# Second layer: value projection with gated weights and the gate's diagonal; VectorE adds the residual base

## Chip, core and metric

The kernel runs on one core of one Trainium2 chip. The metric is the device time of one execution in microseconds. The engines are TensorE (PE, matmuls into PSUM; PEld is its weight load), VectorE (DVE), ScalarE (ACT), GpSimd (POOL), and SyncE, whose queue (SPq) issues the DMAs.

## What is computed

Two transformer layers over x of 32 sequences, 256 tokens, 128 features, float32. The part that the change touches is the attention of the second layer:

```python
h = _layernorm(x, axis=-1) * (1 + ca) + sa
x = x + ga * _L1_attn_ref(h, ...)          # ga, ca, sa: one row of 128 for each sequence

def _L1_attn_ref(x, ln_scale, ln_bias, wq, wk, wv):
    xn = _layernorm(x, ln_scale, ln_bias)
    q, k, v = ((xn @ w) split in 16 heads of 8 for w in (wq, wk, wv))
    probs = softmax(q @ k.T / sqrt(128))
    return heads_joined(probs @ v) + xn    # the residual inside the attention is xn
```

So with x as it enters the layer, the new x is x + ga·(probs @ v) + ga·xn. The first layer has another attention (an output projection, a slope bias, no inner residual). A mixture of experts follows each attention; its input rows are written by token to a table in DRAM.

## The kernel before

The program has five blocks in time: setup (constants, the modulation rows of both layers), attention of layer 0, experts 0, attention of layer 1, experts 1. An attention block is a software pipeline over the 32 sequences. One **tick** `i` works on several sequences at once: `at(off)` is sequence `i + off`. Each engine has a hand-written order of steps within a tick (`tick` in each engine's block); the first and the last ticks are peeled, the middle runs in a loop of two ticks. Engines wait for each other by counting semaphores. A `Signal` is one such count, and `after(b)` is its value once sequence `b` is through.

TensorE's tick has 16 score passes `scores_a` (L1093, one for each head, into the two PSUM tiles `A`), of which VectorE takes the row maxima (`row_max`, L849). Pass h may start when maximum h - 2 has been taken. Between the passes stand the transposed scores `scores_b` (L1117), the sums `weigh` (L1132) and small steps that share the one PSUM bank `M0`: `project_qk` (L1076, L1077), `project_v` (L1081), transposes, router products. ScalarE takes the exponentials (L701) and reads `M0` into SBUF; `values` (L686) reads the projected values.

The attention of layer 1 has these steps around the change:

- GpSimd `add_experts` (L577 to L579) makes X, the input of layer 1, from the first layer's rows; it runs three sequences ahead.
- VectorE `outer_norm` (the L803 group that writes xn from X, two instructions), `modulate_rows` (L832, L834) and `inner_norm` (L803, xn from xn) make the normalised rows, two sequences ahead. TensorE turns them; ScalarE applies `ln_scale` and `ln_bias` and writes hT, the transposed xn of the reference.
- GpSimd `split_qk` (L567 to L570, four instructions of 512 columns) and then `residual_base` (L588 to L591, four of 256 columns) run one sequence ahead. `residual_base` computes X + ga·(xn·ln_scale + ln_bias) into `xh`; `store_base` (L490) sends it to DRAM and `load_back` (L485) brings it back as `XR` when it is needed.
- VectorE `residual` (L890, L892), two sequences behind, computes h3 = On·ga + XR, where On holds the attention's output.

The SP queue issues, in a fixed order in each tick, 12 DMAs of 64 KB for the score stacks (`stack<-parts`, L498), 2 for the maxima (`stack<-mrow`, L504), and the loads and stores of rows. It waits in order: what stands behind a waiting issue waits too.

Of the kernel before, what the change touches and what calls it, by code (L numbers as in the profile page):

```python
# [40 lines left out]
DVE_MARKS = (36, 42)  # L41
# [81 lines left out]
def build(nc, a, out):  # L123
    with ExitStack() as ctx:
# [6 lines left out]
        def dram(name, shape, dt=F32):  # L131
# [4 lines left out]

        x_mid = [dram(f"x_mid{n}", (B * S, D)) for n in range(3)]
# [19 lines left out]
        wo = sb("wo", [P, P])  # L157
        qk_bias = sb("qk_bias", [P, 2])
# [46 lines left out]
        xh = [sb(f"xh{u}", [P, NT, D]) for u in range(2)]  # L205
        gb_row = [sb(f"gb_row{u}", [P, 1, D]) for u in range(2)]
        lnrow = sb("lnrow", [P, 2, D])
# [53 lines left out]
            (ln_cols[:, :], a["ln_cols"]), (lnrow[:, :, :], a["ln_rows"].broadcast_to([P, 2, D])), (gate_w[:, :, :], a["gate_w"]), (cT[:, :, :], a["cT"]),  # L261
# [130 lines left out]
def attention(nc, l, g):  # L392

    (X, XR, X1, st, mv, rs, xn, hT, qk, rem, parts, stack, vals, mx, mneg, mrow, probs, heads, rsum, On, OnT, yT,
     st2, mv2, rs2, xn2, front_rows, back_rows, xh, qs_bias, h2, h3, h2T, eps_col, lg, rt, r1, sel, slot_in, token_ids, run) = (g[n] for n in (
        "X XR X1 st mv rs xn hT qk rem parts stack vals mx mneg mrow probs heads rsum On OnT yT "
        "st2 mv2 rs2 xn2 front_rows back_rows xh qs_bias h2 h3 h2T eps_col lg rt r1 sel slot_in token_ids run").split())
# [6 lines left out]
    gb_row, ones_col, lnrow, Y, expert_out, XR, a, w1, w2, b1, b2 = (g[n] for n in  # L404
        "gb_row ones_col lnrow Y expert_out XR a w1 w2 b1 b2".split())
# [19 lines left out]
    back_in = transfers("back_in", 2)  # L425
    base_out = transfers("base_out", 1)
# [30 lines left out]
    with nc.Block() as block:  # L457

        @block.sync
        def _(sp):  # L460
# [7 lines left out]
            def load_front(b, k, u):  # L468
# [3 lines left out]
                else:  # L472
                    sp.wait_ge(base_ready.handle, base_ready.after(b - 2))
# [3 lines left out]
                    sp.dma_start(front_rows[u][:, :, :], mod_of(1, b, SA, 3)).then_inc(front_in[u], 16)  # L477
# [1155 lines left out]
```

## Time and profile before

| | |
|---|---|
| median of 3 runs | 2274.51 us (2273.72 to 2276.03) |
| profiled execution, its own time | 2273.52 us |
| its span in the trace | 2271.7 us |
| busy share PE / DVE / ACT / POOL | 79% / 75% / 46% / 42% |
| setup | 0 to about 41 us |
| attention 0 | about 42 to 890 us |
| experts 0 | about 890 to 1137 us |
| attention 1 | about 1155 to 2000 us |
| experts 1 | about 2020 to 2271 us |

How to read what is quoted: a window row gives start and end, then the busy time of PE, PEld, DVE, ACT and POOL in this order, each with its count of instructions, then the granted TensorE clock as a share of full speed, the busy share of the DMA engines, and GB/s. A group row gives a line of the kernel, the engine, the operation, its output and inputs with shapes, the count, the busy time, the mean in ns, and the idle time just before. A timeline row gives start and duration in us; "x2" means that the row stands for two instructions in a row, and a bracket is idle time before it and who ended it.

### The profile page before, as it was taken

How to read it: one execution, taken by the hardware profiler on the slowest of the kernel's cores; microseconds unless marked ns; L12 is line 12 of the kernel's file. 1: busy time of each engine (PE TensorE's matmuls, PEld its weight loads, DVE VectorE, ACT ScalarE, POOL GpSimd, SP SyncE). 2: the span in 40 equal slices, each digit the busy share in tenths (PEclk: the TensorE clock that was granted, in tenths of full speed). 3: DMA queues.
4: the chain of work that ended last, by engine and by line, in shares of the span. 5: the costliest groups of instructions: out<-in, count | busy, mean ns of one | idle time of the engine just before them, and what ended most of it. 6: DMA issues, size and time to landing. Idle time of an engine off the chain costs nothing. (4 is left out here: it accounts for less than half of the span.)

```text
span 2271.7 us, 57921 instructions
## 1 busy us (share of the span) xinstructions
PE 1787.5 (79%) x15650; PEld 1288.8 (57%) x15650; DVE 1694.5 (75%) x5861; ACT 1039.5 (46%) x1967; POOL 951.4 (42%) x1028
## 2 busy tenths in 40 slices
PE   1699999999999929999906777777777777719997
PEld 1466666666667618999803444444444444407776
DVE  3488888888888746666627988998999899824453
ACT  0266666666666612222204555555555555602322
POOL 0233444343444324454425455445545554313433
PEclk7699999999999969999957999999999998959999
DMA  3334444444444332222235443544444444343332
GB/s 125 48 69 70 75 74 76 70 76 71 75 73 73 61 72 59 71 69 67 60 115 90 100 98 91 98 101 100 94 99 98 96 96 95 70 141 96 100 92 62
DMA packets 260822, 191.15 MB, mean 84 GB/s; under 512 B 24824, under 2 KB 251002, under 8 KB 260046
## 3 DMA queue, kind: packets, MB, share of 16 engines
q1 hardware_dynamic: 245402, 155.40, 33.2%
q0 software_dynamic: 15360, 35.03, 5.4%
q8 instruction: 28, 0.46, 0.1%
q14 instruction: 32, 0.26, 0.1%
HBM read 95.37 MB, written 53.15 MB: 65 GB/s over the span
## 5 line engine op out<-in xcount | busy, mean ns | idle before, releaser
L849 DVE TENSOR_REDUCE mx<-A 128x2 f32<-128x512 f32 x1024 | 692.6, 683 | 127.5 <-PE A L1097 51.1
L701 ACT ACTIVATE probs<-B 128x1024 f32<-128x1024 f32 x512 | 524.0, 1023 | 350.4 <-PE B L1120 180.8
L1093 PE MATMUL A<-stack 126*128 126x256 bf16 x2048 | 440.7, 287 | 159.6 <-DVE mx L849 127.9
L1117 PE MATMUL B<-stack 128*128 128x256 bf16 x2048 | 364.1, 281 | 31.8 <-DMA stack<-mrow 31.6
L1093 PEld LDWEIGHTS A<-stack 126*128 126x128 bf16 x2048 | 180.8, 100 | 328.9 <-DVE mx L849 244.4
L1132 PE MATMUL M<-probs,vals 128*32 128x256 f32 x4096 | 289.1, 399 | 21.6 <-DVE On L875 17.4
L611 POOL DMA_INDIRECT gathered<-h,slot_in x192 | 187.2, 975 | 155.2 <-DVE slot_in L988 109.6
L1117 PEld LDWEIGHTS B<-stack 128*128 128x128 bf16 x2048 | 203.4, 103 | 83.2 <-issue 31.2
L598 POOL TENSOR_TENSOR h<-xn,back_rows 128x256 f32<-128x256 f32 x64 | 46.4, 724 | 465.6 <-DVE xn L803 465.6
L1533 PE MATMUL A<-w2s,hid 128*128 128x128 f32 x1792 | 230.5, 279 | 9.0 <-issue 9.0
L1533 PEld LDWEIGHTS A<-w2s,hid 128*128 128x128 f32 x1792 | 211.9, 192 | 18.3 <-issue 13.3
L1524 PE MATMUL B<-xtT,w1s 128*128 128x256 f32 x896 | 216.3, 395 | 6.0 <-DVE xtT L1410 2.8
L1339 POOL DMA_INDIRECT expert_out<-yt,row_dest x144 | 138.1, 959 | 177.7 <-DVE yt L1445 143.4
L1097 PE MATMUL A<-dist,slope_ident 128*128 128x128 bf16 x1024 | 201.2, 222 | 0.0
L1524 PEld LDWEIGHTS B<-xtT,w1s 128*128 128x128 f32 x896 | 168.3, 195 | 40.5 <-issue 17.1
L1132 PEld LDWEIGHTS M<-probs,vals 128*32 128x32 f32 x4096 | 125.1, 112 | 103.4 <-issue 43.4
L1120 PE MATMUL B<-dist,slope_ident 128*128 128x128 bf16 x1024 | 183.1, 219 | 0.0
L1493 ACT ACTIVATE hid<-B 128x1024 f32<-128x1024 f32 x72 | 73.7, 1024 | 228.7 <-PE B L1524 228.7
L567 POOL TENSOR_TENSOR parts<-qk,ones_col 128x512 bf16<-128x512 f32 x64 | 66.5, 1039 | 258.8 <-ACT qk L680 112.5
L708 ACT ACTIVATE heads<-M 128x256 f32<-128x256 f32 x256 | 97.9, 382 | 147.7 <-PE M L1132 146.7
L1336 POOL DMA_INDIRECT out<-yt,row_dest x80 | 84.5, 1056 | 169.7 <-DVE yt L1450 146.2
L1497 ACT ACTIVATE hid<-B,b 128x256 f32<-128x256 f32 x160 | 62.6, 474 | 173.4 <-PE B L1524 138.0
(193 smaller groups left out, 3079.2 us busy)
## 6 DMA issues: line engine op xcount, KB each, us to landing
stack<-parts SPq DMA_DIRECT2D x768, 64.0 KB
xt<-gathered SPq DMA_DIRECT2D x112, 132.0 KB, 2.2
back_rows<-mod_rows SPq DMA_DIRECT2D x64, 192.0 KB, 3.4
probs<-gathered SPq DMA_DIRECT2D x40, 256.0 KB, 2.7
w<-in_w SPq DMA_DIRECT2D x4, 2048.0 KB
Y<-expert_out SPq DMA_DIRECT2D x64, 128.0 KB
front_rows<-mod_rows SPq DMA_DIRECT2D x32, 192.0 KB
X<-in_x SPq DMA_DIRECT2D x32, 128.0 KB, 3.2
```

What stands on the lines that cost most here:

```text
L611: pool.indirect_dma_start(gathered[l], bass.IndirectOffsetOnAxis(ap=slot_in[u][:, c, t:t + 1], axis=0), (h3 if l else h2)[u][:, t, :], Non ...
L701: act.activation(probs[c % 4][:, :, :, :], Bp[c % 2][:, :, :, :], ACT.Exp, scale=EXP_SCALE[l][c // 4]).then_inc(b_exp.handle, 1)
L708: act.activation(heads[g % 2][:, :], M1[:, 0:S], ACT.Copy).then_inc(o_read.handle, 1)
L849: dve.tensor_reduce(mx[u][:, h, :], A[h % 2][:, :, :], AX.X, ALU.max).then_inc(a_max.handle, 1)
L1093: ins = pe.matmul(A[h % 2][:, t, :], stack[u][0:n, h, 0, t * P:(t + 1) * P], stack[u][0:n, h, 1, :], start=True, stop=(l == 1))
L1097: ins = pe.matmul(A[h % 2][:, t, t * P:(t + 1) * P], slope_ident[:, h % HH, :], dist[:, t, :], start=False, stop=True)
L1117: ins = pe.matmul(Bp[c % 2][:, j, t, :], stack[u][:, h, 1, t * P:(t + 1) * P], stack[u][:, h, 0, :], start=True, stop=(l == 1))
L1120: ins = pe.matmul(Bp[c % 2][:, j, t, t * P:(t + 1) * P], slope_ident[:, h % HH, :], dist[:, 1 - t, :], start=False, stop=True)
L1132: ins = pe.matmul(M1[VW * j:VW * j + VW, 0:S], vals[u][:, t, 4 * g + j, :], probs[(2 * g + j // 2) % 4][:, j % 2, t, :], start=(t == 0), s ...
L1339: ins = pool.indirect_dma_start(expert_out[l], dest, yt[u][:, t, :], None)
L1524: ins = pe.matmul(dst[:, f, :], w1s[u][:, f * P:(f + 1) * P], xtT[u][:, :], start=True, stop=True)
L1533: ins = pe.matmul(A[u][:, t, 0:D], hid[u][:, f, t * P:(t + 1) * P], w2s[u][:, f, :], start=(f == 0), stop=(l == 0 and f == FC - 1))
```

## The change

`residual_base`, `store_base` and the tiles `xh` and `lnrow` go. In their place:

- **Setup**: the gate rows ga go to a DRAM table `gate_rows` of 32 x 256, the right half in plain order, the left half in the order in which the heads stand (three DMAs at the end of the setup block, and a wait for them). A constant `wv_id` of 128 x 256 (wv beside the identity) is loaded instead of `lnrow`.
- **SP queue**: `load_ga` brings the row of a sequence, broadcast to 128 partitions; `store_x2` sends X to DRAM and `load_x2` brings it back as `XR`, in place of `xh`. `back_rows` and `front_rows` lose a row each.
- **GpSimd** `gate_values`: one product of 128 x 256, `wv_ga = wv_id * ga_rows`: the value weights and the identity with every column multiplied by ga.
- **TensorE** `project_v`: 256 columns instead of 128 for each half of the sequence. `M0` then holds ga·v and beside it ga·xn, and all 512 columns are in use.
- **VectorE** `gated_base`: xb = XR + the right halves of `M0`, after `modulate_rows`. `residual` becomes one addition, On + xb. TensorE's next users of `M0` (`count`, `turn_max`) wait for `base_ready` instead of `v_ready`.

```diff
@@ setup, SP queue
+                sp.dma_start(gate_rows[:, D:2 * D], mod_sb[:, GA * D:(GA + 1) * D]).then_inc(gates_out, 16)
+                for f in range(2):
+                    sp.dma_start(gate_rows[:, f * (D // 2):(f + 1) * (D // 2)].rearrange("b (h d) -> b h d", d=HD),
+                                 mod_sb[:, GA * D:(GA + 1) * D].rearrange("b (h f d) -> b f h d", f=2, d=HD)[:, f, :, :])\
+                        .then_inc(gates_out, 16)
+                sp.wait_ge(gates_out, 48)
...
@@ attention, SP queue
-                    sp.wait_ge(base_ready.handle, base_ready.after(b - 2))
+                    sp.wait_ge(h_rows.handle, h_rows.after(b - 2))
+                    sp.wait_ge(x2_out[u], x2_out.of(k - 1))
                     sp.dma_start(X[u][:, :, :], rows_of(x_view[1], b)).then_inc(x_in[u], 16)
...
-                if l == 1:
-                    sp.wait_ge(base_out[u], base_out.of(k))
-                sp.dma_start(XR[u][:, :, :], rows_of(x_view[2 * l], b)).then_inc(back_in[u], 16)
-                sp.dma_start(back_rows[u][:, :, :], mod_of(l, b, GA, 3)).then_inc(back_in[u], 16)
-
-            def store_base(b, k, u):
-                sp.wait_ge(base_ready.handle, base_ready.after(b))
-                sp.dma_start(rows_of(x_view[2], b), xh[u][:, :, :]).then_inc(base_out[u], 16)
+                if l == 0:
+                    sp.dma_start(XR[u][:, :, :], rows_of(x_view[0], b)).then_inc(back_in[u], 16)
+                sp.dma_start(back_rows[u][:, 1:3, :], mod_of(l, b, SB, 2)).then_inc(back_in[u], 16)
+
+            def store_x2(b, k, u):
+                sp.wait_ge(x2_ready.handle, x2_ready.after(b))
+                sp.dma_start(rows_of(x_view[2], b), X[u][:, :, :]).then_inc(x2_out[u], 16)
+
+            def load_x2(b, k, u):
+                sp.wait_ge(base_ready.handle, base_ready.after(b - 2))
+                sp.wait_ge(x2_out[u], x2_out.of(k))
+                sp.dma_start(XR[u][:, :, :], rows_of(x_view[2], b)).then_inc(x2_in[u], 16)
+
+            def load_ga(b, k, u):
+                sp.wait_ge(wv_ready.handle, wv_ready.after(b - 2))
+                sp.dma_start(ga_rows[u][:, :], gate_rows[bass.ds(b, 1), :].broadcast_to([P, 2 * D])).then_inc(ga_in[u], 16)
...
                     stack_max(*at(-1), 1)
+                if l and at(2):
+                    store_x2(*at(2))
+                    load_ga(*at(2))
                 if at(-1):
                     load_back(*at(-1))
...
                 if l and at(1):
-                    store_base(*at(1))
+                    load_x2(*at(1))
...
@@ attention, GpSimd
-            def residual_base(b, k, u):
-
-                def row(n, x):
-                    return x[:, n:n + 1, :].broadcast_to([P, NT, D])
-                pool.wait_ge(xn_ready.handle, xn_ready.after(b))
-                pool.wait_ge(base_out[u], base_out.of(k - 1))
-                h = xh[u][:, :, :]
-                ch.link(pool.tensor_tensor(h, xn[u][:, :, :], row(0, lnrow), ALU.mult))
-                ch.link(pool.tensor_tensor(h, h, row(1, lnrow), ALU.add))
-                ch.link(pool.tensor_tensor(h, h, row(GA, front_rows[u]), ALU.mult))
-                pool.tensor_tensor(h, h, X[u][:, :, :], ALU.add).then_inc(base_ready.handle, 1)
+            def gate_values(b, k, u):
+                pool.wait_ge(ga_in[u], ga_in.of(k))
+                pool.wait_ge(v_proj.handle, v_proj.after(b - 2))
+                pool.tensor_tensor(wv_ga[u][:, :], wv_id[:, :], ga_rows[u][:, :], ALU.mult).then_inc(wv_ready.handle, 1)
...
@@ attention, VectorE
+            def gated_base(b, k, u):
+
+                dve.wait_ge(x2_in[u], x2_in.of(k))
+                dve.wait_ge(v_ready.handle, v_ready.after(b))
+                dve.wait_ge(x1_ready.handle, x1_ready.after(b - 2))
+                dve.tensor_tensor(xb[u][:, :, :], XR[u][:, :, :],
+                                  M0[:, :].rearrange("p (t n) -> p t n", t=NT)[:, :, D:2 * D], ALU.add)\
+                    .then_inc(base_ready.handle, 1)
+
             def residual(b, k, u):
...
-                    x3 = x1_of(u)
-                    ch.link(dve.tensor_tensor(x3, On[u][:, :, :, :].rearrange("p t h d -> p t (h d)"),
-                                              back_rows[u][:, 0:1, :].broadcast_to([P, NT, D]), ALU.mult))
-                    dve.tensor_tensor(x3, x3, XR[u][:, :, :], ALU.add).then_inc(x1_ready.handle, 1)
+                    dve.tensor_tensor(x1_of(u), On[u][:, :, :, :].rearrange("p t h d -> p t (h d)"), xb[u][:, :, :],
+                                      ALU.add).then_inc(x1_ready.handle, 1)
...
                 layer(1, modulate_rows, 2)
+                layer(1, gated_base, 0)
                 maxima(9, 1)
...
@@ attention, TensorE
             def project_v(b, k, u):
+                if l:
+                    pe.wait_ge(wv_ready.handle, wv_ready.after(b))
+                n, w = (2 * D, wv_ga[u][:, :]) if l else (D, wv[:, l, :])
                 for t in range(NT):
-                    ins = pe.matmul(M0[:, t * P:(t + 1) * P], hT[u][:, t * P:(t + 1) * P], wv[:, l, :],
-                                    start=True, stop=True)
+                    ins = pe.matmul(M0[:, t * n:(t + 1) * n], hT[u][:, t * P:(t + 1) * P], w, start=True, stop=True)
                 ins.then_inc(v_proj.handle, 1)
...
-                    m0_read(*[(x1_ready, -2)] * (l == 0), (v_ready, 0), (mT_read, -1, 2))
+                    m0_read(*[(x1_ready, -2)] * (l == 0), (base_ready if l else v_ready, 0), (mT_read, -1, 2))
...
-                    m0_read((pos_read, -3), *[(x1_ready, -2)] * (l == 0), (v_ready, 0))
+                    m0_read((pos_read, -3), *[(x1_ready, -2)] * (l == 0), (base_ready if l else v_ready, 0))
```

VectorE in the middle of a tick, before the change, from the residual (L890, L892) over two row maxima (L849) and statistics (h is the tile that takes the new x, mv and rs are mean and reciprocal deviation) to `outer_norm` (L803):

```order
L890 TENSOR_TENSOR h<-On,back_rows 128x2x128
L892 TENSOR_TENSOR h<-h,XR 128x2x128
L849 TENSOR_REDUCE mx<-A 128x2
L798 BN_STATS st<-h 128x6 x2
L849 TENSOR_REDUCE mx<-A 128x2
L789 BN_AGGR mv<-st 128x2 x2
L803 TENSOR_SCALAR xn<-X,mv,rs 128x128 x2
L856 TENSOR_SCALAR mneg<-mx 128x2x8
```

The same place after it (the line numbers are now those of the changed kernel):

```order
L916 TENSOR_TENSOR h<-On,xb 128x2x128
L867 TENSOR_REDUCE mx<-A 128x2
L817 BN_STATS st<-h 128x6 x2
L867 TENSOR_REDUCE mx<-A 128x2
L808 BN_AGGR mv<-st 128x2 x2
L822 TENSOR_SCALAR xn<-X,mv,rs 128x128 x2
L874 TENSOR_SCALAR mneg<-mx 128x2x8
```

One instruction has gone, and the others keep their order. A little later on VectorE, before, where the heads' output is normalised (On) and `modulate_rows` (L832, L834) is followed by the tenth row maximum:

```order
L871 RECIPROCAL rsum<-M 128x8
L875 TENSOR_TENSOR On<-M,rsum 128x2x4x8
L832 TENSOR_TENSOR xn<-xn,front_rows 128x256
L834 TENSOR_TENSOR xn<-xn,front_rows 128x256
L849 TENSOR_REDUCE mx<-A 128x2
L943 TENSOR_SCALAR h<-token_ids 128x2
```

And after:

```order
L889 RECIPROCAL rsum<-M 128x8
L893 TENSOR_TENSOR On<-M,rsum 128x2x4x8
L850 TENSOR_TENSOR xn<-xn,front_rows 128x256
L852 TENSOR_TENSOR xn<-xn,front_rows 128x256
L906 TENSOR_TENSOR xb<-XR,M 128x256
L867 TENSOR_REDUCE mx<-A 128x2
L969 TENSOR_SCALAR h<-token_ids 128x2
```

The new addition L906 stands ahead of the maximum. GpSimd's tick before, from the last two instructions of the split (parts and rem hold q and k and what bf16 leaves over) on:

```order
L569 TENSOR_TENSOR parts<-rem,ones_col 128x2x256
L99 REGISTER_ALU
L570 TENSOR_TENSOR parts<-rem,parts 128x2x256
L586 REGISTER_ALU
L588 TENSOR_TENSOR xh<-xn,lnrow 128x256
L99 REGISTER_ALU
L589 TENSOR_TENSOR xh<-xh,lnrow 128x256
L99 REGISTER_ALU
L590 TENSOR_TENSOR xh<-xh,front_rows 128x256
L99 REGISTER_ALU
L591 TENSOR_TENSOR xh<-xh,X 128x256
```

And after:

```order
L594 TENSOR_TENSOR parts<-rem,ones_col 128x2x256
L99 REGISTER_ALU
L595 TENSOR_TENSOR parts<-rem,parts 128x2x256
L607 ISA
L608 REGISTER_ALU
L609 TENSOR_TENSOR wv_ga<-wv_id,ga_rows 128x256
L613 REGISTER_ALU
L614 ISA
```

Of four instructions behind the split, one is left.

## Rows read from the trace of the kernel before

**Rows 1.** windows: start:end, length, busy us (count) each engine, PEclk, DMA

```profile
150.00:900.00 750.00, 665.54 (x7052) 493.78 (x7049) 615.78 (x2138) 422.22 (x771) 309.03 (x318) 0.97 0.40 71
...
1200.00:1900.00 700.00, 520.86 (x4445) 308.10 (x4445) 626.85 (x2009) 386.21 (x771) 361.46 (x418) 0.93 0.45 96
```

**Rows 2.** waits, 1250 to 1900 us: total us, times, longest us

```profile
PE A L1093 <- DVE mx L849: 89.1, 135, 1.7
...
DVE mx L849 <- PE A L1093: 32.0, 53, 0.7
```

**Rows 3.** DVE groups, 1250 to 1900 us: count, busy us, mean ns, idle us

```profile
L849 DVE TENSOR_REDUCE mx<-A 128x2 f32<-128x512 f32 x417 | 280.7, 678 | 35.4 <-PE A L1093 32.0
L803 DVE TENSOR_SCALAR xn<-X,mv,rs 128x128 f32<-128x128 f32 x52 | 39.4, 798 | 3.4
L890 DVE TENSOR_TENSOR h<-On,back_rows 128x256 f32<-128x256 f32 x26 | 32.5, 1251 | 1.4
L892 DVE TENSOR_TENSOR h<-h,XR 128x256 f32<-128x256 f32 x26 | 29.8, 1146 | 0.9
```

**Rows 4.** timeline of DVE in one tick: start us, duration us, instruction

```profile
1440.78 1.13 DVE L890 TENSOR_TENSOR h<-On,back_rows 128x256 f32<-128x256 f32 x1
1441.94 1.15 DVE L892 TENSOR_TENSOR h<-h,XR 128x256 f32<-128x256 f32 x1
1443.01 0.68 DVE L849 TENSOR_REDUCE mx<-A 128x2 f32<-128x512 f32 x1
...
1444.95 1.52 DVE L803 TENSOR_SCALAR xn<-X,mv,rs 128x128 f32<-128x128 f32 x2
...
1447.97 0.42 DVE L834 TENSOR_TENSOR xn<-xn,front_rows 128x256 f32<-128x256 f32 x1
```

**Rows 5.** timeline of POOL in the same tick

```profile
1440.47 1.16 POOL L568 TENSOR_TENSOR rem<-qk,parts 128x512 f32<-128x512 f32 x1
1441.70 1.10 POOL L569 TENSOR_TENSOR parts<-rem,ones_col 128x512 bf16<-128x512 f32 x1
1442.88 1.22 POOL L570 TENSOR_TENSOR parts<-rem,parts 128x512 bf16<-128x512 f32 x1
...
1444.86 0.72 POOL L589 TENSOR_TENSOR xh<-xh,lnrow 128x256 f32<-128x256 f32 x1
1445.67 0.72 POOL L590 TENSOR_TENSOR xh<-xh,front_rows 128x256 f32<-128x256 f32 x1
```

**Rows 6.** line 892, whole trace: durations min/median/max ns; its second last tick

```profile
L892 DVE TENSOR_TENSOR h<-h,XR x32: 424/1145/1273, 1242.9 to 1992.8; 128x256 f32<-128x256 f32 x32
...
1978.56 0.42 DVE L892 TENSOR_TENSOR h<-h,XR 128x256 f32<-128x256 f32 x1
```

**Rows 7.** lines 803 and 896 in the first layer, same columns

```profile
L803 DVE TENSOR_SCALAR xn<-X,mv,rs x106: 334/340/576, 202.8 to 812.7; 128x128 f32<-128x128 f32 x106
...
L896 DVE TENSOR_TENSOR X<-XR,M x28: 409/410/421, 219.7 to 809.3; 128x256 f32<-128x256 f32 x28
```

**Rows 8.** timeline of PE: a 256-column projection, and the tick of rows 4

```profile
1412.28 0.70 PE L1076 MATMUL M<-hT,wq 128*128 128x256 f32 x2
...
1442.78 0.61 PE L1081 MATMUL M<-wv,hT 128*128 128x128 f32 x4
...
1447.21 0.39 PE L1093 MATMUL A<-stack 126*128 126x256 bf16 x2 [1.65 <-DVE mx L849]
```

**Rows 9.** timeline of ACT in the tick of rows 4

```profile
1443.90 0.38 ACT L686 ACTIVATE vals<-M 128x256 f32<-128x256 f32 x1
```

**Rows 10.** waits of the SP queue, 1250 to 1900 us, and its stack issue

```profile
SPq L504 <- ACT mrow L694: 252.8, 52, 5.0
...
1419.48 4.00 SPq L498 DMA_DIRECT2D stack<-parts  x6
```

**Rows 11.** end of setup: timeline

```profile
38.70 0.33 SPq L281 DMA_DIRECT2D mod_rows<-mod_sb  x1
...
41.76 1.28 ACT L643 ACT_TABLE_LOAD   x1 [25.93 <-PEq L271]
```

More of the change, by code:

```diff
@@ L40 @@
 EPS_IN = 1e-6
-DVE_MARKS = (36, 42)
+DVE_MARKS = (36, 41)
 MIDST = (2, 4, 5, 7, 8, 10, 11, 13, 14)
@@ L204, in build @@
         back_rows = [sb(f"back_rows{u}", [P, 3, D]) for u in range(2)]
-        xh = [sb(f"xh{u}", [P, NT, D]) for u in range(2)]
+        xb = [sb(f"xb{u}", [P, NT, D]) for u in range(2)]
         gb_row = [sb(f"gb_row{u}", [P, 1, D]) for u in range(2)]
-        lnrow = sb("lnrow", [P, 2, D])
+        ga_rows = [sb(f"ga_rows{u}", [P, 2 * D]) for u in range(2)]
+        wv_ga = [sb(f"wv_ga{u}", [P, 2 * D]) for u in range(2)]
         h2 = [sb(f"h2{u}", [P, NT, W]) for u in range(2)]
@@ L403, in attention @@
         "before_tri ones_b rev_iota mod_rows gathered x_view region_row".split())
-    gb_row, ones_col, lnrow, Y, expert_out, XR, a, w1, w2, b1, b2 = (g[n] for n in
-        "gb_row ones_col lnrow Y expert_out XR a w1 w2 b1 b2".split())
+    gate_rows, ga_rows, wv_ga, wv_id = (g[n] for n in "gate_rows ga_rows wv_ga wv_id".split())
+    gb_row, ones_col, Y, expert_out, XR, a, w1, w2, b1, b2 = (g[n] for n in
+        "gb_row ones_col Y expert_out XR a w1 w2 b1 b2".split())
     n_choice = CHOICES[l]
@@ L424, in attention @@
     front_in = transfers("front_in", 4)
-    back_in = transfers("back_in", 2)
-    base_out = transfers("base_out", 1)
+    back_in = transfers("back_in", 1 if l else 2)
+    x2_out = transfers("x2_out", 1)
+    x2_in = transfers("x2_in", 1)
+    ga_in = transfers("ga_in", 1)
     stack_in = Transfers([[sem(f"stack_in{u}{h}") for h in range(2)] for u in range(2)], len(PRODUCTS))
@@ L523, in _ @@
                 sp.wait_ge(lin_in, 32)
-            for t in (x_in, stack_in, m_in, x1_out, front_in, back_in, base_out, gate_in):
+            for t in (x_in, stack_in, m_in, x1_out, front_in, back_in, x2_out, x2_in, ga_in, gate_in):
                 t.start(sp)
@@ L551, in _ @@
             for u in range(2):
-                sp.wait_ge(*((base_out[u], base_out.of(B // 2 - 1)) if l else (x1_out[u], x1_out.of(B // 2 - 1))))
+                sp.wait_ge(*((x2_in[u], x2_in.of(B // 2 - 1)) if l else (x1_out[u], x1_out.of(B // 2 - 1))))
         @block.gpsimd
         def _(pool):
-            start(pool, split, h2_ready, scattered, *([base_ready, x2_ready] if l else []))
+            start(pool, split, h2_ready, scattered, *([wv_ready, x2_ready] if l else []))
             ch = Chain(pool, pool_order)
@@ L632, in tick @@
                     scatter_done(*at(-3))
-            run_ticks(pool, tick, ch, 10 if l else 5)
+            run_ticks(pool, tick, ch, 7 if l else 5)
         @block.scalar
@@ L780, in _ @@
             if l == 1:
-                start(dve, h_rows, h_stats, rms_stats, h3_ready)
+                start(dve, h_rows, h_stats, rms_stats, h3_ready, base_ready)
             ch = Chain(dve, dve_order)
@@ L826, in outer_norm @@
                 dve.wait_ge(xn_T.handle, xn_T.after(b - 2))
-                dve.wait_ge(base_ready.handle, base_ready.after(b - 2))
                 normed(X[u], mv[u], rs[u], xn[u], h_rows)
```

27 lines of the change are left out of this document (16 added, 11 removed).

## The prediction, made before the changed kernel was timed

> **What bounds the kernel now.** First the windows [rows 1]. In the attention of layer 1 VectorE is busy 626.85 of 700 us (90%), TensorE 74%, ScalarE 55%, GpSimd 52%. A tick is short to see: 417 row maxima in 650 us [rows 3], 16 to a tick, make 26.1 ticks, so 24.9 us each. Then the waits [rows 2]: in this stretch TensorE waits 89.1 us for row maxima, VectorE 32.0 us for scores. So the tick is VectorE's list of work, with TensorE close behind in places. The change touches only this block and the end of setup; layer 0 loses one row of 64 KB from a load that nobody waits for.
>
> Then the groups of VectorE [rows 3]. Two instructions of 256 columns in `residual`, L890 and L892, take 1251 and 1146 ns each, and the two of 128 columns in `outer_norm` (L803 from X) 798 ns. The same shapes are much cheaper elsewhere: L892 takes 0.42 us in the last ticks, where GpSimd has no split [rows 6], and L803 a median of 340 ns in layer 0 [rows 7]. The two timelines beside each other say why [rows 4, 5]: L890 starts at 1440.78, while GpSimd's L568 runs until 1441.63, and ends at 1441.91, 0.28 behind it. L892 ends at 1443.09, 0.29 behind L569 (1442.80). The pair of `outer_norm` starts at 1444.95 inside L589 (until 1445.58) and ends at 1446.47, just behind L590 (1446.39). Each of these four instructions stands until the GpSimd instruction beside it is over. The row maxima keep their 678 ns. What an edit to either engine is worth hangs on who meets whom.
>
> **The change part by part.** The sum is made against the profiled execution, 2273.52 us (span 2271.7 and 1.8 around it), which is 1.0 us below the median.
>
> *L892 goes.* In rows 4 the next maximum starts at 1443.01, 0.08 before the end of L892. Behind L890 alone (end 1441.91) it would start at 1441.83: 1.18 us earlier. Its operands are there: its score pass stands before the heads' product in TensorE's order. What is left of `residual` starts where L890 did and meets the same L568, so it keeps its 1.13 us. Of the 32 instructions I count 29 as blocked and 3 at 0.46 with the gap (the last ticks, [rows 6]): 29 x 1.18 + 3 x 0.46 = 35.6 us less.
>
> *`outer_norm` meets other GpSimd work.* It starts 1.18 earlier, at 1443.77. L570 then still runs, until 1444.10 at the latest [rows 5], perhaps 0.1 less since nothing pushes it. Behind it GpSimd now has one product of 256 columns, to be priced as L589: 0.72 us, from 1444.08 to 1444.80. So the first half of `outer_norm` waits for L570, the second for the product, and the pair ends about 0.08 behind it, at 1444.88: 1.11 us instead of 1.52, 0.41 less. The bounds: nothing gained (1.52 again), or both free, 2 x 0.34 with an overlap [rows 7], 0.9 less. I take 0.41, as the four starts in rows 4 and 5 fix it. In 29 ticks: 11.9 us less.
>
> *`gated_base` is added.* The nearest row is L896 of layer 0: the same shape, one operand in SBUF and one in PSUM, 410 ns with a spread of 409 to 421 [rows 7]. With the spacing of such a step 0.44 us, 32 times: 14.1 us more. If it too were held up by a GpSimd instruction it would take what L892 takes, 1.15 us, and 29 x 0.74 = 21.5 us more again. I take the lower: it comes just behind L834 (end 1448.39, [rows 4], now about 1.6 earlier), and GpSimd would be idle from 1444.80 on. The Trainium skill ("SBUF — State Buffer", section "Who interferes with whom") says that a VectorE instruction with two SBUF inputs contends with a GpSimd instruction that reads SBUF, and one with at most one SBUF input outside the two-port modes does not. By that rule the 21.5 us can't come even if the two meet; rows 3 to 5 agree with its first half, and no row here shows the second, since I found L896 beside no GpSimd arithmetic.
>
> Does `gated_base` wait? It needs `values` of ScalarE, which ended at 1444.28 [rows 9]. The wider projection makes that later: L1081 took 0.61 us for two tiles of 128 columns, L1076 0.70 for one of 256 [rows 8], so two take at most 1.40: at most 0.8 later, 1445.1. VectorE comes to it at about 1446.8. No wait. Its other inputs come from transfers a tick older.
>
> *TensorE.* Those 0.8 us stand between `scores_b` and the ninth score pass. In rows 8 the projection starts at 1442.78, so it ends by 1444.18, and the pass (0.39 us) by 1444.57. The maximum that reads it was taken behind `outer_norm`, which now ends at 1444.88. Hidden, by 0.3 us; before the change TensorE had 1.65 us of idle two passes on [rows 8]. The new wait of `count` and `turn_max` for `base_ready` costs nothing: VectorE has passed `gated_base` before it takes the tenth maximum, and both stand behind a score pass that needs the eleventh.
>
> *GpSimd* loses three instructions of 0.72 us in each tick. It is no bound; the only worth of it is in `outer_norm`, above.
>
> *The SP queue* issues one transfer more in each tick (x2 out and in for base out and in, and the gate row), some 0.35 to 0.5 us, ahead of the stack issue of 4.00 us [rows 10]. The queue stands idle 4.9 us twice in each tick before a `stack<-mrow` (252.8 us over 52, [rows 10]): covered. `store_x2` makes the queue wait for `add_experts`, with the stack rows of the next sequence behind it; GpSimd has done that at the end of the tick before.
>
> *Setup.* The last transfer of the modulation rows is issued at 38.70, and attention 0 begins at 41.76 [rows 11]: 3.06 us from issue to the next block. Three more are issued only after its landing, 0.33 each at the least and, in pieces of 8 elements, 0.67 each as one stack transfer (4.00 over six, [rows 10]), and must land: about 1.7 + 2.3 = 4.0 us more, between 2.5 and 8. Nothing else runs there.
>
> Sum: -35.6 - 11.9 + 14.1 + 4.0 = -29.4 us; 2273.5 - 29.4 = 2244.1, by the median 2245.
>
> **The rivals.**
>
> A. As above, with the bounds of `outer_norm`: nothing gained there gives 2257, all of it (29 x 0.49 more) 2231. Chance 0.68.
>
> B. More than that. TensorE's long wait of 1.65 us shrinks, and its clock, granted at 0.93 on average in this block [rows 1], stays high; VectorE's own 32 us of waits [rows 2] is then halved: 16 less, 2215 to 2230. For it: the idle does shrink. Against: most of these waits are elsewhere in the tick. Chance 0.08.
>
> C. VectorE gives the time back. The stretch from the heads' product to the ninth pass is full of TensorE work, and the margin found above is 0.3 us. If the pass comes 0.5 us later than worked out, 0.2 to 0.5 of the 1.15 us a tick is lost, or `gated_base` is blocked (0.74 a tick): 2257 to 2270. Chance 0.13.
>
> D. The change doesn't do what it says: the gain of a tick is eaten, because TensorE's path, not VectorE, sets the time from L890 to the ninth pass. Then L892's going is worth nothing there, and what is left is +0.44 and -0.41 a tick and the setup: 2270 to 2279, within 0.2%. Against: TensorE waits for a maximum at both ends of this stretch. Chance 0.05.
>
> E. Slower. The same place, with TensorE the bound behind the wider projection: +0.8 us a tick for it, and nothing from L892 and `outer_norm`: 32 x 0.8 - 3 + 4 = +27, with `gated_base` hidden in VectorE's new idle; 2290 to 2310. It decides once the ninth pass ends later than VectorE asks for it; it stands 0.4 us short of that by the numbers above, and would have to come 1.5 us later to use up the gain. For it: the stretch has no gap in TensorE. Against: the 1.65 us. Chance 0.06.
>
> **How the numbers follow.** About 0.2% (4.5 us) is what a measurement of this kernel can tell from no change. Faster by more: A, B and C, 0.89, less a little for a C that reaches 2270: 0.88. Same: D with that remainder, 0.06. Slower: 0.06. The range is 2228, just inside B, to 2263, half-way through C: it holds A whole and parts of both, some 0.8.
>
> **What would show it.** In the groups of VectorE: no L892, the one instruction of `residual` at 1.1 to 1.25 us still, `outer_norm` at some 0.55 us each, `gated_base` at 0.41 without a wait before it. The tick, from one residual to the next over two ticks, 23.8 us instead of 24.9. VectorE still at 90%, TensorE at 80% with its waits for maxima down. Attention 0 begins at some 45.8. The prediction is wrong if VectorE's idle before maxima grows by what its work shrinks (C, D, E), if `outer_norm` keeps 798 ns (A's upper end), or if `gated_base` stands for `values` or takes over 1 us.

## Result, and the profile after

The changed kernel takes 2248.83 us (median of 4 runs, 2240.77 to 2250.82) against 2274.95 us beside it: ratio 0.9879 (95% interval 0.9853 to 0.9904), 26 us less. Two later comparisons on other occasions gave 0.9867 (0.9852 to 0.9882) and 0.9872 (0.9855 to 0.9888). The forecast was 2245, with 2228 to 2263.

The profiled execution took 2240.77 us, the least of the four, with a span of 2239.0: 32.7 us below the span of before. Measured by the starts of the `residual` instruction over 26 ticks in the middle of attention 1, a tick fell from 24.99 to 23.84 us.

The window of attention 1, as in [rows 1] (660 us, since the block is shorter):

```profile
1200.00:1860.00 660.00, 508.50 (x4389) 299.66 (x4387) 584.46 (x1989) 379.73 (x761) 292.80 (x327) 0.95 0.51 102
```

VectorE is busy 584.46 of 660 us (89%), TensorE 77% instead of 74%, GpSimd 44% instead of 52%. The waits, as in [rows 2], over 600 us instead of 650:

```profile
PE A L1122 <- DVE mx L867: 65.2, 98, 0.9
...
DVE mx L867 <- PE A L1122: 32.3, 51, 0.9
```

TensorE's waits for row maxima fell from 3.4 to 2.6 us a tick; VectorE's waits for scores are 1.28 us a tick, where they were 1.23. VectorE is the bound as before, of a shorter list. VectorE's groups, as in [rows 3], 1250 to 1850 us:

```profile
L867 DVE TENSOR_REDUCE mx<-A 128x2 f32<-128x512 f32 x404 | 271.6, 677 | 32.5 <-PE A L1122 32.3
L916 DVE TENSOR_TENSOR h<-On,xb 128x256 f32<-128x256 f32 x25 | 32.2, 1287 | 0.6
L822 DVE TENSOR_SCALAR xn<-X,mv,rs 128x128 f32<-128x128 f32 x50 | 27.6, 591 | 1.5
...
L852 DVE TENSOR_TENSOR xn<-xn,front_rows 128x256 f32<-128x256 f32 x25 | 10.6, 425 | 0.9
L906 DVE TENSOR_TENSOR xb<-XR,M 128x256 f32<-128x256 f32 x25 | 10.5, 421 | 5.7 <-DVE xn L852 5.7
```

The residual's one instruction (L916) is held up as L890 was, 1287 ns against 1251. `outer_norm` (L822 from X) fell from 798 to 591 ns. `gated_base` (L906) takes 421 ns; the 0.23 us of idle time before it (5.7 over 25 of them) are put down to VectorE's own L852, so it waited for no other engine. One tick of VectorE, as in [rows 4]:

```profile
1621.13 1.17 DVE L916 TENSOR_TENSOR h<-On,xb 128x256 f32<-128x256 f32 x1
1622.22 0.68 DVE L867 TENSOR_REDUCE mx<-A 128x2 f32<-128x512 f32 x1
...
1624.10 1.10 DVE L822 TENSOR_SCALAR xn<-X,mv,rs 128x128 f32<-128x128 f32 x2
...
1626.70 0.43 DVE L852 TENSOR_TENSOR xn<-xn,front_rows 128x256 f32<-128x256 f32 x1
1627.35 0.42 DVE L906 TENSOR_TENSOR xb<-XR,M 128x256 f32<-128x256 f32 x1 [0.23 <-DVE xn L852]
1627.69 0.68 DVE L867 TENSOR_REDUCE mx<-A 128x2 f32<-128x512 f32 x1
```

And GpSimd in the same tick, as in [rows 5]:

```profile
1620.86 1.16 POOL L593 TENSOR_TENSOR rem<-qk,parts 128x512 f32<-128x512 f32 x1
1622.09 1.10 POOL L594 TENSOR_TENSOR parts<-rem,ones_col 128x512 bf16<-128x512 f32 x1
1623.27 1.16 POOL L595 TENSOR_TENSOR parts<-rem,parts 128x512 bf16<-128x512 f32 x1
1624.39 0.72 POOL L609 TENSOR_TENSOR wv_ga<-wv_id,ga_rows 128x256 f32<-128x256 f32 x1
```

L916 ends at 1622.30, 0.28 behind L593 (1622.02). `outer_norm` starts at 1624.10 inside L595 (until 1624.43) and ends at 1625.20, 0.09 behind the gate product (1625.11); from single instructions, its first half ends 0.08 behind L595 and its second 0.08 behind the product. From the start of L852 to the start of the next maximum it is 0.99 us (1626.70 to 1627.69). Before, without `gated_base`, it was 0.55 from L834 (1447.97, [rows 4]) to the maximum behind it:

```profile
1448.52 0.69 DVE L849 TENSOR_REDUCE mx<-A 128x2 f32<-128x512 f32 x1
```

So `gated_base` adds 0.44. TensorE and ScalarE in the same tick, as in [rows 8, 9]:

```profile
1623.13 1.03 PE L1111 MATMUL M<-wv_ga,hT 128*128 128x256 f32 x4
1623.99 0.38 PE L1122 MATMUL A<-stack 126*128 126x256 bf16 x2
...
1625.93 0.39 PE L1122 MATMUL A<-stack 126*128 126x256 bf16 x2 [0.61 <-DVE mx L867]
```

```profile
1624.25 0.38 ACT L706 ACTIVATE vals<-M 128x256 f32<-128x256 f32 x1
```

The projection L1111 takes 1.03 us for 0.61, and the ninth pass starts at 1623.99 behind it with no wait for VectorE. `values` ends at 1624.63, 2.7 us before `gated_base`. The end of setup, as in [rows 11]:

```profile
38.84 0.33 SPq L285 DMA_DIRECT2D mod_rows<-mod_sb  x1
...
40.63 0.32 SPq L287 DMA_DIRECT2D gate_rows<-mod_sb  x1
40.98 0.92 SPq L289 DMA_DIRECT2D gate_rows<-mod_sb  x2
44.36 1.28 ACT L661 ACT_TABLE_LOAD   x1 [28.50 <-PEq L275]
```

The three gate transfers are issued from 40.63 to 41.90, and the block begins at 44.36 instead of 41.76. In the other traces of kernels with this setup it begins between 43.69 and 44.11.

### The profile page after: what moved, and what is told of

Same layout as the page of the kernel before. It is cut to its first block and busy times, and to the rows that moved or that the text cites. A ratio compares the mean times of both kernels' runs of the same rounds, so it can differ in the third digit from the quotient of the medians.

```text
span 2239.0 us, 57857 instructions
## 1 busy us (share of the span) xinstructions
PE 1779.3 (79%) x15650; PEld 1283.3 (57%) x15650; DVE 1652.0 (74%) x5861; ACT 1039.1 (46%) x1967; POOL 881.2 (39%) x932
## 5 line engine op out<-in xcount | busy, mean ns | idle before, releaser
L1122 PE MATMUL A<-stack 126*128 126x256 bf16 x2048 | 433.2, 283 | 136.2 <-DVE mx L867 102.5
L1146 PE MATMUL B<-stack 128*128 128x256 bf16 x2048 | 357.7, 277 | 32.6 <-DMA stack<-mrow 32.4
L1146 PEld LDWEIGHTS B<-stack 128*128 128x128 bf16 x2048 | 197.2, 101 | 84.3 <-issue 30.6
```

What stands on the lines that cost most here:

```text
L1122: ins = pe.matmul(A[h % 2][:, t, :], stack[u][0:n, h, 0, t * P:(t + 1) * P], stack[u][0:n, h, 1, :], start=True, stop=(l == 1))
L1146: ins = pe.matmul(Bp[c % 2][:, j, t, :], stack[u][:, h, 1, t * P:(t + 1) * P], stack[u][:, h, 0, :], start=True, stop=(l == 1))
```

## Experiments

Each was timed beside the kernel before on the same chip; "tick" is the mean over 26 middle ticks, read from its trace as above. The first four ran on another chip, where every kernel takes some 130 us more: the kernel before 2407.34 us. Most of that lies in layer 0, whose attention ended at 958 to 962 us in the four traces of that chip, instead of 832 to 835; the cause was not looked for. (The table ahead of the change puts the end of attention 0 at about 890. In the trace of before its last row maximum ends at 787.5, and VectorE's first instruction of experts 0 starts at 831.9; that is the point meant here.) Attention 1 is alike there (a variant of the changed kernel, e4 below, has a tick of 23.88 us), so ticks can be compared, and times only as ratios.

**The kernel before without L890 (e1).**

```diff
-                    ch.link(dve.tensor_tensor(x3, On..., back_rows..., ALU.mult))
-                    dve.tensor_tensor(x3, x3, XR[u][:, :, :], ALU.add).then_inc(x1_ready.handle, 1)
+                    dve.tensor_tensor(x3, On..., XR[u][:, :, :], ALU.add).then_inc(x1_ready.handle, 1)
```

This leaves the gate out of the attention's part. (Operands are cut to `...`.)

> The kernel before with one edit: the product On*ga (L890) is left out, so the residual is the single addition On + XR; GpSimd's four instructions of the residual base stay. Theory (each of VectorE's two-input or two-port instructions stands until the GpSimd instruction beside it ends, and the tick is VectorE's list): the residual loses one instruction of 1.18 us a tick (35 us), and outer_norm, which then starts 1.18 us earlier, waits for L570 and for L588 alone instead of L589 and L590: 1.11 us for its pair instead of 1.52, 12 us more; 2227 us. Rival 1 (outer_norm got shorter because GpSimd's list did): it keeps 1.5 us and the time is 2239. Rival 2 (TensorE sets this stretch): above 2260.

Measured: 2383.03 us, ratio 0.9910 (0.9892 to 0.9929), 24 us less; tick 24.16, so 0.83 less and not 1.6. The groups of VectorE, 1350 to 1950 us:

```profile
L890 DVE TENSOR_TENSOR h<-On,XR 128x256 f32<-128x256 f32 x24 | 30.3, 1262 | 1.3
L803 DVE TENSOR_SCALAR xn<-X,mv,rs 128x128 f32<-128x128 f32 x50 | 26.6, 572 | 3.0
...
L834 DVE TENSOR_TENSOR xn<-xn,front_rows 128x256 f32<-128x256 f32 x25 | 21.0, 839 | 0.9
...
L832 DVE TENSOR_TENSOR xn<-xn,front_rows 128x256 f32<-128x256 f32 x25 | 18.8, 752 | 0.0
```

The two things expected are there: one residual instruction at 1262 ns, and `outer_norm` at 572 ns with all four GpSimd instructions in place, so rival 1 falls: it got shorter because it comes earlier. But `modulate_rows` (L832, L834) takes 752 and 839 ns: VectorE, ahead by 1.6 us, has run into L590 and L591. Before, from 1250 to 1900 us:

```profile
L834 DVE TENSOR_TENSOR xn<-xn,front_rows 128x256 f32<-128x256 f32 x26 | 11.0, 425 | 0.9
L832 DVE TENSOR_TENSOR xn<-xn,front_rows 128x256 f32<-128x256 f32 x26 | 10.8, 415 | 0.0
```

That is 0.75 us a tick more: 1.18 + 0.45 - 0.75 = 0.88, for 0.83 measured.

**The kernel before with one GpSimd instruction as residual base (e2).**

```diff
-                ch.link(pool.tensor_tensor(h, xn[u][:, :, :], row(0, lnrow), ALU.mult))
-                ch.link(pool.tensor_tensor(h, h, row(1, lnrow), ALU.add))
-                ch.link(pool.tensor_tensor(h, h, row(GA, front_rows[u]), ALU.mult))
-                pool.tensor_tensor(h, h, X[u][:, :, :], ALU.add).then_inc(base_ready.handle, 1)
+                pool.tensor_tensor(h, xn[u][:, :, :], X[u][:, :, :], ALU.add).then_inc(base_ready.handle, 1)
```

This leaves the scale, bias and gate out of the base. 

> The kernel before with one edit: GpSimd's residual base is one instruction of 256 columns (xn + X) instead of four; VectorE's list is untouched. Theory: the residual keeps its 1.13 to 1.38 and 1.15 us, but outer_norm, which starts 0.15 us after that one instruction has ended, runs free at 0.6 us for the pair instead of 1.52: 0.9 us a tick, 26 us less, 2249 us. Rival (a lighter GpSimd list is worth nothing): 2275 us. In between, 0.3 to 0.6 us a tick, if the one instruction still touches the pair: 2258 to 2266.

Measured: 2383.02 us, ratio 0.9908 (0.9890 to 0.9926); tick 24.16, 0.83 less. The same groups:

```profile
L887 DVE TENSOR_TENSOR h<-On,back_rows 128x256 f32<-128x256 f32 x25 | 30.5, 1220 | 1.4
L889 DVE TENSOR_TENSOR h<-h,XR 128x256 f32<-128x256 f32 x24 | 27.5, 1146 | 0.8
...
L800 DVE TENSOR_SCALAR xn<-X,mv,rs 128x128 f32<-128x128 f32 x50 | 16.3, 369 | 3.0
```

The residual is as it was, and `outer_norm` takes 369 ns, 0.86 us a tick less. Nothing was taken from VectorE's list: GpSimd instructions that GpSimd had ample time for cost VectorE 0.86 us a tick where they met it.

**More GpSimd products beside `gated_base`, in the changed kernel (e3).**

```diff
+                for _ in range(5):
+                    ch.link(pool.tensor_tensor(beside[:, :], wv_id[:, :], wv_id[:, :], ALU.mult))
```

(`beside` is a tile of its own that nothing reads.)

> The changed kernel with five more GpSimd products of 256 columns (0.72 us each, SBUF to SBUF, result unused) behind the gate product, so that GpSimd computes from 1624.4 to about 1629.2 in the tick shown, over modulate_rows and gated_base. Theory (two SBUF inputs are held up, one in SBUF and one in PSUM is not): L850 and L852 take about 0.7 to 0.9 us each instead of 0.42, gated_base (L906) keeps 0.41 to 0.43; some 0.75 us a tick, 22 us more than the changed kernel, 2271 us. Rival (gated_base is held up too): L906 at 0.7 to 1.1 us and 2280 to 2290 us.

Measured: 2405.15 us, ratio 1.0004 (0.9988 to 1.0019), against 0.988 for the changed kernel: 30 us more (by the ratios; e4 below, which takes what the changed kernel does, took 2375.35 us on this chip); tick 24.94, 1.10 more. That is more than the 22 us of the theory and close to the rival's, so the groups have to decide. VectorE's groups, then the five products of one tick on GpSimd, then VectorE beside them:

```profile
L877 DVE TENSOR_SCALAR mneg<-mx 128x16 bf16<-128x16 f32 x49 | 20.4, 417 | 4.2 <-issue 4.0
...
L855 DVE TENSOR_TENSOR xn<-xn,front_rows 128x256 f32<-128x256 f32 x25 | 18.0, 719 | 0.9
L853 DVE TENSOR_TENSOR xn<-xn,front_rows 128x256 f32<-128x256 f32 x25 | 16.0, 642 | 0.0
...
L909 DVE TENSOR_TENSOR xb<-XR,M 128x256 f32<-128x256 f32 x25 | 10.5, 422 | 5.3 <-DVE xn L855 5.3
```

```profile
1720.11 3.50 POOL L612 TENSOR_TENSOR beside<-wv_id 128x256 f32<-128x256 f32 x5
```

```profile
1722.42 0.72 DVE L855 TENSOR_TENSOR xn<-xn,front_rows 128x256 f32<-128x256 f32 x1
1723.37 0.42 DVE L909 TENSOR_TENSOR xb<-XR,M 128x256 f32<-128x256 f32 x1 [0.23 <-DVE xn L855]
```

L853 and L855 take 642 and 719 ns instead of 415 and 425, as expected, and L877, a small product on the row maxima that I had not thought of, 417 on average instead of 198. It runs twice a tick: the one beside these products takes 0.60 us instead of 0.16, the other is as it was. Together that is 0.95 of the 1.10 us.

L909, with one operand in PSUM, keeps 422 ns. In the tick shown it starts at 1723.37 inside the last product (until 1723.61), and if it had been held up like L853 and L855 (which end 0.28 behind their product) it would have taken 0.52. In four ticks near the ends of the block it lies wholly inside a product, as here:

```profile
1353.67 0.67 POOL L612 TENSOR_TENSOR beside<-wv_id 128x256 f32<-128x256 f32 x1
```

```profile
1353.91 0.42 DVE L909 TENSOR_TENSOR xb<-XR,M 128x256 f32<-128x256 f32 x1
```

Held up, it would have ended at 1354.62 and taken 0.71; it ended at 1354.33, before the product did. No L909 of the 32 took more than 422. So the rival falls. The Trainium skill ("SBUF — State Buffer", section "Who interferes with whom"), which the prediction cited, says that a VectorE instruction with at most one SBUF input, outside the two-port modes, does not contend; these four ticks agree. The trace of before could have shown it too: 38 of the 104 instructions L875 (On from M in PSUM and rsum in SBUF, 1250 to 1900 us) lie wholly inside a GpSimd product and take 218 ns on average, and the 26 beside an idle GpSimd 224. But one SBUF input alone does not make an instruction free: `outer_norm` and L877 read a single large tile from SBUF (the mean, the deviation and the factor are one value a row) and are held up, while the statistics L798, which also read one tile, keep 273 ns beside GpSimd's split. No run here shows what sets them apart.

**The projection at 128 columns, in the changed kernel (e4).**

```diff
-                n, w = (2 * D, wv_ga[u][:, :]) if l else (D, wv[:, l, :])
+                n, w = (2 * D, wv_ga[u][:, 0:D]) if l else (D, wv[:, l, :])
...
-                    ins = pe.matmul(M0[:, t * n:(t + 1) * n], hT[u][:, t * P:(t + 1) * P], w, start=True, stop=True)
+                    ins = pe.matmul(M0[:, t * n:t * n + D], hT[u][:, t * P:(t + 1) * P], w, start=True, stop=True)
```

> The changed kernel with the value projection at 128 columns again (only the left half of wv_ga is used); gated_base still reads the right halves of M0, which are then stale. This leaves ga*xn out of the result. It prices the wider projection. Theory (hidden under outer_norm): within 3 us of the changed kernel, 2249 us, with TensorE's waits for row maxima up by what it no longer computes, about 0.4 us a tick. Rival (TensorE bounds the stretch up to the ninth pass): 0.4 us a tick or more less, 2237 us or below.

Measured: 2375.35 us, ratio 0.9878 (0.9858 to 0.9898), the changed kernel's own on the other chips; tick 23.88 for 23.84. TensorE's waits in 600 us:

```profile
PE A L1122 <- DVE mx L867: 69.5, 103, 1.2
```

69.5 us for 65.2, 0.17 us a tick more and not 0.4: part of what TensorE no longer computes became wait for VectorE. The wider projection costs nothing that shows, so the mechanism of cases D and E is not there.

**The changed kernel again, and its spread (e5).**

> The changed kernel as it is, as the yardstick for the three beside it and for its own spread (2240.8 to 2250.8 so far): 2249 us, 0.988 of the kernel before. If the spread comes from TensorE's clock in the first 150 us, the trace shows layer 0 longer by the difference and attention 1 at the same 810 us.

Measured: 2245.91 us, ratio 0.9867 (0.9852 to 0.9882). Its profiled execution took 2246.79, 6.0 more than the first, and the guess on the spread was wrong: attention 0 ended at the same time (833.4 against 833.6 us). From the first to the last `residual` it took 721.3 us, where the first profile took 717.6. The windows, first profile and this one:

```profile
1250.00:1850.00 600.00, 463.82 (x4051) 273.76 (x4049) 536.06 (x1860) 350.15 (x704) 268.65 (x300) 0.96 0.51 103
```

```profile
1250.00:1850.00 600.00, 483.68 (x4040) 284.82 (x4033) 534.38 (x1847) 349.61 (x702) 266.85 (x298) 0.90 0.50 102
```

TensorE's granted clock was 0.96 in the one and 0.90 in the other. In the middle that costs little: ticks of 24.06 us stand among those of 23.8 in this one, 1.1 us over 25 ticks. The rest lies at the ends of the block: the first tick took 23.8 us for 22.2, and the last but one 19.3 for 17.7 (the other ticks there give 0.6 back). The run e9 below, the changed kernel once more, is slower by 1.6 us in each of two ticks near the end; this is the first of them, in the first profile and in e9's:

```profile
1907.36:1927.16 19.80, 15.59 (x158) 9.88 (x155) 17.34 (x60) 12.13 (x22) 7.67 (x9) 1.00 0.43 80
```

```profile
1908.52:1929.90 21.38, 17.16 (x158) 10.38 (x155) 17.35 (x60) 12.16 (x22) 7.66 (x9) 0.92 0.40 76
```

VectorE works the same 17.3 us in both. TensorE works 15.59 us at a granted clock of 1.00 and 17.16 at 0.92, and the tick is 1.6 us longer: where the pipeline empties, TensorE has a part in the pace. Another 2 us were lost before the block. So the first profile flatters the change; this one gives 26.7 us less than before.

**The gate product later, the setup transfers together, and both (e6, e7, e8).**

```diff
+                if l and at(-2):
+                    modulate(*at(-2))
                 if l and at(1):
                     gate_values(*at(1))
-                if l and at(-2):
-                    modulate(*at(-2))
```

```diff
                     sp.dma_start(mod_rows[l], mod_sb[:, :]).then_inc(mod_out, 16)
-                    sp.wait_ge(mod_out, 16 * (l + 1))
+                    if l == 0:
+                        sp.wait_ge(mod_out, 16)
...
+                sp.wait_ge(mod_out, 32)
                 sp.wait_ge(gates_out, 48)
```

> The changed kernel with the gate product (L609) moved behind GpSimd's modulate in the tick, where GpSimd is idle. Theory: outer_norm then meets only the end of L595: the first half still waits for it, the second runs free, 0.87 us for the pair instead of 1.10; 0.23 us a tick, 7 us less: 2242 us. Rival (the product costs nothing where it is, another wait takes its place): 2249 us. Rival (behind modulate it holds up other two-input instructions): above 2249 us.

Measured: 2233.66 us, ratio 0.9819 (0.9806 to 0.9832), 12.3 us below the changed kernel beside it; tick 23.42, 0.43 less. The pair fell to 0.68 us, not 0.87: one tick of it, then the group, whose mean is that of a single instruction:

```profile
1619.81 0.68 DVE L822 TENSOR_SCALAR xn<-X,mv,rs 128x128 f32<-128x128 f32 x2
```

```profile
L822 DVE TENSOR_SCALAR xn<-X,mv,rs 128x128 f32<-128x128 f32 x50 | 16.9, 377 | 1.5
```

That is 0.43 us a tick less (twice 591 - 377 ns), all that the tick lost. In its new place the product meets only row maxima and the statistics L938 (286 ns, as before), so the second rival falls too.

> The changed kernel with the three gate transfers issued right behind the last modulation transfer, without waiting for its landing. Theory: the 2.5 us that setup grew by shrink to about 0.9 (three issues of 0.33 and 0.46 us), so 1.5 us less, 2247.5 us; attention 0 begins at 42.8 instead of 44.4. Rival: the landing of the small pieces sets it, and nothing changes.

Measured: 2246.38 us, ratio 0.9870 (0.9855 to 0.9885). The block begins at 42.84 us, 1.3 to 1.5 us earlier than in the two profiles of the changed kernel so far (44.11, 44.36), as expected, but the time shows nothing of it: it is below the spread.

```profile
42.84 1.28 ACT L663 ACT_TABLE_LOAD   x1 [27.24 <-PEq L275]
```

> Both edits, the later product and the transfers together: 7 + 1.5 us less than the changed kernel, 2240.5 us, if both theories hold.

Measured: 2230.96 us, ratio 0.9803 (0.9790 to 0.9817). This computes the whole result and is the fastest such kernel of the study, 15 us below the changed kernel beside it, where 8.5 were expected; beside the later product alone, the transfers add no gain that is clear of the spread.

**Three more GpSimd products, with a yardstick (e9 the yardstick, e10 the products).**

> The changed kernel as it is, as the yardstick on this chip: 0.987 of the kernel before, a tick of 23.84 us.

Measured: 2247.02 us, ratio 0.9872 (0.9855 to 0.9888), tick 23.84.

The next is the loop of the third experiment with `range(3)`. 

> The changed kernel with three more GpSimd products of 256 columns (result unused) behind the gate product, so that GpSimd's list is as long as that of the kernel before while VectorE's is the changed one. Theory from the run without L890: with VectorE ahead by 1.2 us, four GpSimd instructions reach into modulate_rows, whose two instructions then take 0.7 to 0.85 us instead of 0.42; 0.5 to 0.8 us a tick, 15 to 24 us more than the changed kernel. Rival (what the prediction on record says: GpSimd's shorter list is worth something in outer_norm alone, and outer_norm meets one product either way): no difference.

Measured: 2263.07 us, ratio 0.9941 (0.9924 to 0.9957), 16 us above the yardstick; tick 24.57, 0.72 more. Its groups, then the yardstick's:

```profile
L877 DVE TENSOR_SCALAR mneg<-mx 128x16 bf16<-128x16 f32 x49 | 20.3, 414 | 4.4 <-issue 4.4
...
L853 DVE TENSOR_TENSOR xn<-xn,front_rows 128x256 f32<-128x256 f32 x24 | 15.6, 649 | 0.0
...
L855 DVE TENSOR_TENSOR xn<-xn,front_rows 128x256 f32<-128x256 f32 x24 | 10.2, 425 | 0.8
```

```profile
L850 DVE TENSOR_TENSOR xn<-xn,front_rows 128x256 f32<-128x256 f32 x25 | 10.4, 416 | 0.0
L874 DVE TENSOR_SCALAR mneg<-mx 128x16 bf16<-128x16 f32 x50 | 9.9, 198 | 4.4 <-issue 4.4
```

`outer_norm` is the same in both, 591 and 589 ns. The cost is in L853 (649 for 416) and in L877 (414 for 198 on average of two a tick; the one beside the products takes 0.60 for 0.16): 0.23 + 0.43 = 0.66 of the 0.72 us. So the rival, which is the prediction's own sentence, falls. L855 goes free, where the expectation had it held up too.

**`gated_base` off VectorE (e11).**

```diff
+            def base_copy(b, k, u):
+                act.wait_ge(x2_in[u], x2_in.of(k))
+                act.wait_ge(x1_ready.handle, x1_ready.after(b - 2))
+                act.activation(xb[u][:, :, :], XR[u][:, :, :], ACT.Copy).then_inc(base_ready.handle, 1)
...
                 step(values, 0)
+                layer(1, base_copy, 0)
...
-                layer(1, gated_base, 0)
```

> The changed kernel with gated_base taken off VectorE: ScalarE copies XR to xb behind values instead, and ga*xn is left out of the result. Theory (the tick is VectorE's list, and gated_base costs it 0.44 us): a tick of 23.40 us, 14 us less than the changed kernel. Rival (it stands in time that VectorE would idle): no difference. Rival (ScalarE's copy of some 0.4 us holds up the exponentials): a tick above 23.6 us.

Measured: 2232.61 us, ratio 0.9800 (0.9784 to 0.9816), 14.4 us below the yardstick; tick 23.44, 0.41 less. The instruction of 0.42 us costs what it takes.

**The residual ahead of the sixth maximum (e12).**

```diff
+                if l == 1:
+                    ch.meanwhile = None
                 step(normalise, -2, 3)
+                layer(1, read_logits, -3)
+                layer(1, residual, -2)
                 maxima(5, 1)
-                step(read_logits, -3)
-                layer(1, residual, -2)
+                layer(0, read_logits, -3)
```

(The lines on `meanwhile` keep the sixth maximum from being taken inside `normalise`.)

> The kernel with both edits (product later, setup transfers together; 2231 us, tick 23.42) and one more: in layer 1 the residual stands ahead of the sixth row maximum, so it meets the end of the split's first instruction instead of the second. Theory 1 (outer_norm still has to wait for the end of GpSimd's last split instruction, so time won ahead of it is lost there): residual 0.5 to 0.8 us instead of 1.28, outer_norm 0.2 to 0.3 us longer each, tick within 0.2 us of 23.42. Theory 2 (the list alone counts): the tick falls by 0.5 to 0.8 us, 15 to 24 us less.

Measured: 2233.82 us, ratio 0.9805 (0.9789 to 0.9821), against 0.9803 without this edit; tick 23.51 for 23.42. The groups:

```profile
L824 DVE TENSOR_SCALAR xn<-X,mv,rs 128x128 f32<-128x128 f32 x50 | 33.1, 700 | 1.5
...
L918 DVE TENSOR_TENSOR h<-On,xb 128x256 f32<-128x256 f32 x25 | 13.1, 525 | 0.6
```

The residual takes 525 ns instead of about 1283, 0.76 us a tick, and `outer_norm` 700 instead of 377, which gives 0.65 back. Theory 1 holds: once the product is out of the way, `outer_norm` waits for the end of GpSimd's split, and time won ahead of it is lost there.

## Why the prediction was right, and where not

**The bound.** Right: VectorE's list sets the tick. Taking 0.42 us off it gives 0.41 back (e11), and 0.66 us of delay on it cost 0.72 (e10). It does so in the middle ticks; where the pipeline fills and empties TensorE counts too (below).

**L892 goes, 1.18 us a tick.** Right. L890's successor keeps its wait (1287 ns for 1251), and the next maximum starts 1622.22, 0.08 before its end, as worked out.

**`outer_norm`, 1.52 to 1.11 us.** The size was right: 1.10. e1 gives 572 ns an instruction, where the changed kernel has 591, with all four GpSimd instructions in place, so it is the earlier start and not GpSimd's shorter list that did it. "The only worth of it is in `outer_norm`", the prediction's sentence on GpSimd's three instructions, was wrong: with VectorE early, they are worth nothing there, and about 0.7 us a tick (e10) one step further on, in `modulate_rows` and in the small product on the maxima, which the faster VectorE would otherwise have run into. The sum did not suffer, since it priced the changed kernel and not the parts: with the new list neither of them meets GpSimd. Had the edit to VectorE been made alone, the same method would have forecast twice the true gain, as the expectation for e1 did (47 us for 24). The halves do add up, nearly: 0.83 us a tick for VectorE's alone (e1) and 0.83 for GpSimd's (e2) make 1.66, and both together, without `gated_base`, take 1.55 off the tick (24.99 to 23.44, e11). What was wrong was how the sum was shared out between them.

**`gated_base`, 0.44 us.** Right: 0.99 - 0.55 in the trace, 0.41 by e11. It did not wait, and its price beside GpSimd, the upper bound of 1.15 us, does not apply (e3).

**TensorE, at most 0.8 us more, hidden.** Right: within the bound, 0.42 us more (1.03 for 0.61), and no difference when taken away (e4). Cases D and E had no ground.

**The SP queue, covered.** Right: it still stands idle before `stack<-mrow`, 198.6 us over 50 waits from 1250 to 1850 us, so 4.0 us each instead of 4.9.

**The tick and the block.** 1.18 + 0.41 - 0.44 = 1.15 us was forecast, 24.99 - 23.84 = 1.15 measured. From the first `outer_norm` of the block to VectorE's first instruction of experts 1, 845.3 us became 812.1 in the first profile: 33.2 less, for 33.4 in the sum. That is the best case. The changed kernel's other two profiles (e5, e9) show 815.3 and 815.2, so 30 less. The sum had given each of 29 ticks the full gain; the middle ticks have it in every profile, to 0.05 us, and the ones at the ends can give 3 us of it back. There is one trace of the kernel before, so how much its own ends vary is not known.

**Setup, 4.0 us.** Too high: 2.6 in the first profile, and 1.9 to 2.4 in the others. The three issues took 1.27 us, where 1.7 were worked out from the stack's issues, and the landing behind them was added in full (2.3 us) although it replaced the landing and the block's start that stood there before.

**The total.** The sum with the measured setup would give 2242.7 for the profiled execution, which took 2240.77; the median of its runs is 2248.83, 4 above the forecast, and that of all twelve runs of the changed kernel (with e5 and e9) 2246.8, 2 above. The block gains 3 us less than the sum in two profiles of three, and the setup costs 1.4 to 2.1 less: that the total comes so close is in part luck, two errors of opposite sign. The ends of the block go with TensorE's granted clock (1.00 against 0.92 in the tick shown under e5). This does not explain the spread of the whole: over the twelve runs the mean granted clock does not order the times (2241.84 us at 0.929, 2247.66 at 0.942). The kernel before spreads by 2 to 3 us beside them, the changed one by 4 to 10, but on the slower chip the kernel before spreads by 17. Why was not settled. Case B, a gain from a steadier clock, did not come: VectorE's waits for scores, which it wanted halved, went from 1.23 to 1.28 us a tick.

## What to carry to other kernels

Where VectorE and GpSimd both work out of SBUF, price an edit by laying the two timelines beside each other: an instruction that is held up ends with its neighbour or just behind it, so taking it away gives back the neighbour's length, and shifting the list changes who meets whom further on. An engine with half its time free can still cost the bound engine its full instruction: move its work into its gaps, as the gate product behind `modulate` did for 12 us, before making it shorter. And when a change has two halves, ask of each what the other would do without it.

## What the runs showed of the hardware

- A VectorE instruction that is held up by GpSimd ends a fixed time behind the end of the GpSimd instruction: 0.28 us for the additions and products of 256 columns with both inputs in SBUF (L890, L892, L916, L832, L834; 0.28 to 0.32 in e12), 0.08 us for each half of `outer_norm`, within 0.03 us for the small L877. Two in a row are split: the second waits for GpSimd's next one, if that has started by then.
- Even a 128x16 product with float32 in and bfloat16 out is held up: 0.60 us beside GpSimd's products (e3 and e10) for 0.16. Row maxima and the addition with one operand in PSUM keep their times to some 10 ns.
- In the ticks in which the pipeline empties, a lower granted clock of TensorE costs time: 19.80 us at 1.00, 21.38 at 0.92, with the same work on VectorE. In the middle of the block it hardly does: 0.96 against 0.90, and 1.1 us over 25 ticks.
- One chip of those used took some 130 us more, nearly all of it by the end of attention 0 (958 to 962 us in four traces, for 832 to 835), with attention 1 as on the others; the cause stays open.
